# Gathered rows split one group later, sums over d apart, loads reordered at the start, dense layers begun in chunk 14

## Chip, cores and metric

One NeuronCore of a Trainium2 chip runs the whole program. The metric is the device time of one execution in microseconds (us), the median over the timed runs. TensorE (PE) does the matmuls, VectorE (DVE), ScalarE (ACT) and GpSimd (POOL) the rest; SyncE (SP) issues DMAs.

## What is computed

For 512 batch rows, 39 embedding tables give one row of 16 numbers each. A two-layer cross network (CIN) works on every batch row and every one of the 16 columns d, and its results are summed over d:

```python
e = stack([tbl_f[ids[:, f]] for f in range(39)])            # 512 x 39 x 16
z0 = einsum('bid,bjd->bdij', e, e)                           # 39*39 pairs
cur0 = relu(einsum('bdk,kl->bld', z0.reshape(...), W0))      # 128 outputs
next_h, direct0 = split(cur0, 2)                             # 64 and 64
z1 = einsum('bid,bjd->bdij', e, next_h)                      # 39*64 pairs
cur1 = relu(einsum('bdk,kl->bld', z1.reshape(...), W1))      # 128 outputs
z = sum(concat([direct0, cur1]), over d)                     # 192 features
h = relu(concat([z, dense_ctx]) @ W_top1 + b_top1)           # 208 -> 512
h = relu(h @ W_top2 + b_top2)                                # 512 -> 256
y = h @ W_top3                                               # 256 -> 1
```

## The kernel before

Everything is written by hand: each engine has its own stream of instructions, and semaphores order them. The batch is cut into 16 chunks of 32 rows; a chunk has 32 x 16 = 512 columns, and all matmuls have these as their moving dimension.

**Fetching a chunk.** GpSimd issues ten indirect DMAs per chunk (line 277; called gathers below) into `found[:, b, 2]`, one of three buffers. ACT makes a rounded copy (line 287) and VectorE the remainder (line 393); the two together are called the split of the chunk. SP then writes both and the plain values to a scratch tensor in DRAM (`lay_out`, line 198), reads them back with fields on partitions (`place`, `x_parts`, two DMAs, line 207), and spreads single rows over many partitions (`widen`, `x_wide`, line 217, 13 DMAs per chunk for groups 1 to 4). Each `widen` waits until the product that last read its buffer is done. The split of chunk c + 2 stands in group 0 of chunk c, on ACT and on VectorE.

**First layer of a chunk.** PE adds pairs of fields (`add_up`, line 482), ACT squares the sums (line 296), PE contracts the squares (`contract0`, line 499), in four pieces. ACT evicts the result (`evict0`, lines 303 to 307) into `h` (two copies) and `direct`; VectorE sums `direct` over d (`reduce0`, line 423).

**Second layer of a chunk**, in five groups g = 0 to 4, n = 5c + g counting them over all chunks. VectorE multiplies `h` with the chunk's fields (`multiply`, line 410): group 0 reads them from PSUM, where PE spread them (`spread_out`, line 512), groups 1 to 4 from `x_wide`. For all groups but 2, ACT rounds the product (`high_part`, line 320), VectorE subtracts to get the remainder (`low_part`, line 418), and PE does three passes: `contract1_hi` with two weights (lines 523, 524) and `contract1_lo` (line 531). Group 2 goes in full precision (`contract1_whole`, lines 538 and 542). `z`, `z_hi` and `z_lo` have three buffers. ACT evicts the sum (`evict1`, line 313) and VectorE sums it over d (`reduce1`, line 429). In group n VectorE does `multiply(n + 1)`, then `low_part(n)`; in group 4 both sums over d stand between them. Pieces of the first layer of the next chunks stand between the groups on PE.

**Dense layers.** Three matmul layers on the batch as columns: "early" the first 480, "late" the last 32. The early `hid1_of` (lines 560, 562) stand in groups 2 to 4 of the last chunk and wait for 15 sums over d, the early `hid2_of` (line 571) around the last `contract1_lo`, `y_of` (line 578) behind; then the late columns.

**Start.** ACT's queue issues four weight loads at once, SP's the ids, `w1` and the dense weights. PE fills the time until the first `x_parts` with 30 matmuls that nobody reads (`keep_busy`, line 489).

```python
            for c in range(1, CHUNKS - 1):
                if c + 2 < CHUNKS:
                    bring(c + 2)
                for i in range(len(WIDE)):
                    widen(c + 1, i)
```

## Time and profile before

| | |
|---|---|
| median of 3 timed runs | 441.9 us (439.06 to 444.56) |
| the profiled execution, timed | 437.52 us |
| its span in the profile | 435.7 us |
| granted TensorE clock, mean | 0.978 of full |
| PE busy | 400.6 us (92%) |
| DVE busy | 345.7 us (79%) |
| ACT busy | 226.0 us (52%) |
| POOL busy | 294.6 us (68%) |
| DMA, mean over the span | 185 GB/s |

A timeline row gives the start and the duration in us, the engine, the kernel's line, the operation, output and input, and in brackets how long the engine had been idle before it and what released it. "x4" means that four like instructions are merged. The profiled execution's 437.52 us are its 435.7 us of span and 1.8 us around it.

### The profile page before, as it was taken

What the parts mean: (1) busy time and instruction counts of PE and PEld (TensorE: products, weight loads), DVE (VectorE), ACT (ScalarE), POOL (GpSimd) and SP (SyncE); (2) the same over time, 40 slices, a digit from 0 to 9 for tenths busy, and PEclk for the clock granted to TensorE, in tenths of its full rate; (3) what the DMA queues carried; (4) which work ended last, traced back from release to release, by engine and by line L of the source; (5) the groups of instructions that cost most, each with busy time, mean ns of one, the idle gap of its engine ahead of it and who ended that gap; (6) DMA issues with size and microseconds to landing.
All of it is one profiled execution on the core that took longest, in us unless ns stands there. A gap on an engine that the chain in (4) does not pass through costs nothing.

```text
span 435.7 us, 4074 instructions
## 1 busy us (share of the span) xinstructions
PE 400.6 (92%) x1426; PEld 249.0 (57%) x1426; DVE 345.7 (79%) x196; ACT 226.0 (52%) x224; POOL 294.6 (68%) x164
## 2 busy tenths in 40 slices
PE   0868977999999899999999799999999999997897
PEld 0734634666666546666656356565656565664464
DVE  0305748799999798999998788999999989999800
ACT  3025544474738356564746273847475656553422
POOL 3778889888888888888888888898989800000000
PEclk9989998999999989999999799999999999999999
DMA  8384956496969497878879493959886888992000
GB/s 309 81 218 128 260 135 176 123 247 187 242 165 265 120 262 178 232 199 216 210 214 222 138 281 78 290 137 233 195 253 187 219 218 226 261 253 56 2 0 0
DMA packets 27862, 80.80 MB, mean 185 GB/s; under 512 B 7265, under 2 KB 16225, under 8 KB 20034
## 3 DMA queue, kind: packets, MB, share of 16 engines
q1 hardware_dynamic: 22146, 77.64, 65.9%
q0 software_dynamic: 5120, 1.32, 3.3%
q10 hardware_dynamic: 576, 1.58, 1.1%
q8 instruction: 11, 0.18, 0.2%
q14 instruction: 9, 0.07, 0.1%
HBM read 76.58 MB, written 3.93 MB: 185 GB/s over the span
## 4 chain that ended last, share of the span: by engine, by line
POOL 44%; PE 39%; issue 9%; DMA 3%; DVE 3%; ACT 0%; DVEq 0%
POOL found L277 44%; PE acc L499 7%; PE acc L531 6%; PE acc L524 5%; PE acc L523 5%; PE acc L542 5%; PE sums L482 3%; DMA found<-in_table_dram,rows_sb 2%; PE acc L538 2%; DVE z_lo L418 2%; PE spread L571 2%; DMA ids_sb<-in_ids_dram 1%; PE spread L512 1%; DVE z L410 1%; PE sums L560 1%
## 5 line engine op out<-in xcount | busy, mean ns | idle before, releaser
L277 POOL DMA_INDIRECT found<-in_table_dram,rows_sb x160 | 294.4, 1840 | 53.6 <-issue 48.5
L320 ACT ACTIVATE z_hi<-z 128x2048 fp32r<-128x2048 f32 x64 | 122.4, 1912 | 95.5 <-DVE z L410 95.5
L418 DVE TENSOR_TENSOR z_lo<-z,z_hi 128x2048 fp32r<-128x2048 f32 x64 | 145.8, 2279 | 0.0
L410 DVE TENSOR_TENSOR z<-x_wide,h 128x2048 f32<-128x2048 f32 x64 | 144.8, 2281 | 0.0
L499 PE MATMUL acc<-squares,w 128*128 128x512 f32 (+1 forms) x224 | 110.8, 612 | 0.0
L523 PE MATMUL acc<-z_hi,w_hi 128*128 128x512 f32 x256 | 107.3, 419 | 0.7 <-ACT cur L313 0.7
L524 PE MATMUL acc<-z_hi,w_lo 128*128 128x512 f32 x256 | 101.0, 394 | 0.0
L531 PE MATMUL acc<-z_lo,w_hi 128*128 128x512 f32 x256 | 84.3, 452 | 10.7 <-DVE z_lo L418 10.7
L296 ACT ACTIVATE squares<-sums 128x1024 f32<-128x1024 f32 x64 | 58.4, 913 | 35.5 <-PE sums L482 35.5
L531 PEld LDWEIGHTS acc<-z_lo,w_hi 128*128 128x128 f32 x256 | 47.9, 190 | 36.4 <-issue 15.2
L499 PEld LDWEIGHTS acc<-squares,w 128*128 128x128 f32 (+1 forms) x224 | 41.8, 192 | 28.8 <-issue 24.6
L523 PEld LDWEIGHTS acc<-z_hi,w_hi 128*128 128x128 f32 x256 | 48.7, 190 | 15.6 <-issue 4.1
L524 PEld LDWEIGHTS acc<-z_hi,w_lo 128*128 128x128 f32 x256 | 48.6, 190 | 13.8 <-issue 3.6
L542 PE MATMUL acc<-z,w_sb 128*128 128x512 f32 x96 | 46.6, 622 | 0.0
L482 PE MATMUL sums<-x_parts,select_sb 128*128 128x512 f32 x112 | 39.8, 425 | 6.8 <-DMA x_parts<-x_rows 4.4
L393 DVE TENSOR_TENSOR found<-found 128x160 fp32r<-128x160 f32 x16 | 5.2, 326 | 48.0 <-ACT found L287 48.0
L410 DVE TENSOR_TENSOR z<-spread,h 128x2048 f32<-128x2048 f32 x16 | 36.5, 2284 | 5.5 <-ACT h L304 3.0
L542 PEld LDWEIGHTS acc<-z,w_sb 128*128 128x128 f32 x96 | 17.5, 196 | 29.5 <-issue 29.5
L482 PEld LDWEIGHTS sums<-x_parts,select_sb 128*128 128x128 f32 x112 | 19.9, 190 | 15.9 <-issue 7.1
L313 ACT ACTIVATE cur<-acc 128x512 f32<-128x512 f32 x16 | 9.6, 597 | 33.0 <-PE acc L531 33.0
L429 DVE TENSOR_REDUCE feat_a<-cur 128x32 f32<-128x512 f32 x16 | 10.7, 669 | 12.3 <-ACT cur L313 12.3
L538 PE MATMUL acc<-z,w_sb 64*128 64x512 f32 x32 | 19.9, 703 | 0.0
(44 smaller groups left out, 134.0 us busy)
## 6 DMA issues: line engine op xcount, KB each, us to landing
x_wide<-x_rows SPq DMA_DIRECT2D x64, 512.0 KB, 8.1
x_wide<-x_rows SPq DMA_DIRECT2D x112, 256.0 KB, 9.9
x_parts<-x_rows SPq DMA_DIRECT2D x32, 128.0 KB, 2.6
x_rows<-found SPq DMA_DIRECT2D x16, 240.0 KB, 2.2
x_wide<-x_rows SPq DMA_DIRECT2D x16, 192.0 KB, 7.2
found<-in_table_dram,rows_sb POOLq DMA_INDIRECT x160, 7.6
w_sb<-in_w_dram SPq DMA_DIRECT2D x1, 1280.0 KB, 8.1
x_wide<-x_rows SPq DMA_DIRECT2D x16, 64.0 KB, 6.7
```

The lines of the kernel that those rows point to most:

```text
L277: pool.indirect_dma_start(out=found[:, b, 2, s * D:s * D + D], out_offset=None, in_=table, in_offset=bass.IndirectOffsetOnAxis(ap=rows_sb[ ...
L296: nc.scalar.activation(squares[rows, q % RING0, 0:n, :], sums[rows, 0:n, :], ACT.Square).then_inc(squared, 1)
L320: nc.scalar.activation(z_hi[:, n % RING], z[:, n % RING], ACT.Copy).then_inc(hi_done, 1)
L410: nc.vector.tensor_tensor(z[:, n % RING], x, h[:, c % 2, :].unsqueeze(1).to_broadcast([P, QUADS, N]), ALU.mult).then_inc(multiplied, 1)
L418: nc.vector.tensor_tensor(z_lo[:, n % RING], z[:, n % RING], z_hi[:, n % RING], ALU.subtract).then_inc(lo_done, 1)
L482: last = nc.tensor.matmul(sums[:, a, :], select_sb[:, t, :], x_parts[:, c % BUFS, :], start=True, stop=True)
L499: last = nc.tensor.matmul(acc0[:, :], w0[rows, t, :], squares[rows, q % RING0, a, :], start=(t == 0), stop=(t == T0 - 1))
L523: nc.tensor.matmul(acc1[:, :], w1_hi[:, t, :], z_hi[:, r, a, :], start=(t == 0), stop=False)
L524: last = nc.tensor.matmul(acc1[:, :], w1_lo[:, t, :], z_hi[:, r, a, :], start=False, stop=False)
L531: last = nc.tensor.matmul(acc1[:, :], w1_hi[:, slot1(g) + a, :], z_lo[:, r, a, :], start=False, stop=(g == G - 1 and a == QUADS - 1))
L538: nc.tensor.matmul(acc1[:, :], w1_sb[0:HALF, VT, :], z[0:HALF, r, 0, :], start=False, stop=False)
L542: last = nc.tensor.matmul(acc1[:, :], w1_sb[:, VT + a, :], z[:, r, a, :], start=False, stop=False)
```

## The change

1. **Ids first.** ACT waits for the ids before it issues its four weight loads. The row numbers of chunk 0 are computed by an instruction of their own, and GpSimd starts when that is done.
2. **Parts by two queues.** For chunk 0 the second half of `place` is issued by ACT instead of SP.
3. **First group in halves.** `multiply(0)` and `high_part(0)` are two instructions of 1024 columns each instead of one of 2048, and PE may start on the first half. `keep_busy` runs 36 matmuls instead of 30.
4. **Sums over d apart, splits in group 1.** `reduce0(c + 1)` stays in group 4 but goes behind the low part, `reduce1` goes to group 1, and the split of chunk c + 2 moves from group 0 to group 1 on ACT and VectorE. In chunks 0 and 1 ACT squares before it evicts, and `evict0(1)` comes a group earlier.
5. **Dense layers.** Early is now 448 columns (14 chunks), late 64. `hid1` has a buffer of its own. The early `hid1_of` start in the last group of chunk 14, one per group, then both `hid2_of`; `y_of(early)` comes right after the last `contract1_lo`.

```diff
-        early, late = slice(0, B - CB), slice(B - CB, B)
+        early, late = slice(0, B - 2 * CB), slice(B - 2 * CB, B)
...
-                place(c)
+                place(sp, c, 0)
+
+                if c:
+                    place(sp, c, 1)
...
+            act.wait_ge(ids_in, 16)
             act.dma_start(select_in, select).then_inc(select_in_done, 16)
...
             split(0)
+            place(act, 0, 1)
...
-            high_part(0)
+            act.wait_ge(half_multiplied, 1)
+            nc.scalar.activation(z_hi[:, 0, 0:2], z[:, 0, 0:2], ACT.Copy).then_inc(half_hi_done, 1)
+            act.wait_ge(multiplied, 1)
+            nc.scalar.activation(z_hi[:, 0, 2:], z[:, 0, 2:], ACT.Copy).then_inc(hi_done, 1)
             for c in range(CHUNKS):
                 for g in range(G):
                     n = G * c + g
+                    if g == 0 and c < 2:
+                        square(ND * (c + 1))
                     if g == 0 and c:
                         evict1(c - 1)
-                    if g == 0 and c < 2:
-                        square(ND * (c + 1))
...
-                    if g == (2 if c else 3) and c + 1 < CHUNKS:
+                    if g == 2 and c + 1 < CHUNKS:
                         evict0(c + 1)
-                    if n == 2:
-                        split(2)
-                    if g == 0 and 0 < c < CHUNKS - 2:
+                    if g == 1 and c + 2 < CHUNKS:
                         split(c + 2)
...
-                    if n == 3:
-                        split(2)
                     if n + 1 < G * CHUNKS:
                         multiply(n + 1)
-                    if g == G - 1 and c + 1 < CHUNKS:
-
-                        reduce0(c + 1)
-                        if c:
-                            reduce1(c - 1)
+                    if n == 2:
+                        split(2)
                     if is_v(n):
                         low_part(n)
                     if n == 0:
                         reduce0(0)
-                    if g == 0 and 0 < c < CHUNKS - 2:
+                    if g == 1 and 0 < c < CHUNKS - 2:
                         split(c + 2)
-                    if n == G * (CHUNKS - 1) + 1:
-                        reduce1(CHUNKS - 2)
+                    if g == 1 and c:
+                        reduce1(c - 1)
+                    if g == G - 1 and c + 1 < CHUNKS:
+                        reduce0(c + 1)
...
-                    if c == CHUNKS - 1 and g >= 2:
-                        for m in [[0], [1], [2, 3]][g - 2]:
+                    if n >= G * (CHUNKS - 1) - 1:
+                        m = n - G * (CHUNKS - 1) + 1
+                        if m < M1 // P:
                             hid1_of(m, early)
+                        else:
+                            hid2_of(m - M1 // P, early)
```

The order on VectorE in a chunk of the steady part. Before, from the two sums over d to the next product with `spread` (`found` is the split, `z_lo` a low part, `z` a product):

```order
L423 TENSOR_REDUCE feat_b<-direct 64x32
L429 TENSOR_REDUCE feat_a<-cur 128x32
L418 TENSOR_TENSOR z_lo<-z,z_hi 128x2048
L410 TENSOR_TENSOR z<-x_wide,h 128x2048
L418 TENSOR_TENSOR z_lo<-z,z_hi 128x2048
L393 TENSOR_TENSOR found<-found 128x160
L410 TENSOR_TENSOR z<-x_wide,h 128x2048
L418 TENSOR_TENSOR z_lo<-z,z_hi 128x2048
L410 TENSOR_TENSOR z<-x_wide,h 128x2048 x2
L418 TENSOR_TENSOR z_lo<-z,z_hi 128x2048
L410 TENSOR_TENSOR z<-spread,h 128x2048
```

The change:

```order
L420 TENSOR_TENSOR z<-spread,h 128x2048
L428 TENSOR_TENSOR z_lo<-z,z_hi 128x2048
L433 TENSOR_REDUCE feat_b<-direct 64x32
L420 TENSOR_TENSOR z<-x_wide,h 128x2048
L428 TENSOR_TENSOR z_lo<-z,z_hi 128x2048
L420 TENSOR_TENSOR z<-x_wide,h 128x2048
L428 TENSOR_TENSOR z_lo<-z,z_hi 128x2048
L403 TENSOR_TENSOR found<-found 128x160
L439 TENSOR_REDUCE feat_a<-cur 128x32
L420 TENSOR_TENSOR z<-x_wide,h 128x2048 x2
L428 TENSOR_TENSOR z_lo<-z,z_hi 128x2048
L420 TENSOR_TENSOR z<-spread,h 128x2048
```

The split (`found`) stood behind one product and two low parts after the sums; now it has one more product and one more low part ahead of it. The two sums over d no longer touch: one stands behind the low part of group 4, the other behind the split.

The order on ACT around the split of chunk 2 (`found`), from the last square of chunk 1 (`squares`, 64 rows) to the first work of chunk 1's groups. Before:

```order
L296 ACTIVATE squares<-sums 64x512
L320 ACTIVATE z_hi<-z 128x2048
L287 ACTIVATE found<-found 128x160
L320 ACTIVATE z_hi<-z 128x2048
L303 ACTIVATE h<-acc 64x512
L304 ACTIVATE h<-acc 64x512
L307 ACTIVATE direct<-acc 64x512
L320 ACTIVATE z_hi<-z 128x2048
L313 ACTIVATE cur<-acc 128x512
L296 ACTIVATE squares<-sums 128x1024 x3
```

The change:

```order
L302 ACTIVATE squares<-sums 64x512
L293 ACTIVATE found<-found 128x160
L326 ACTIVATE z_hi<-z 128x2048
L309 ACTIVATE h<-acc 64x512
L310 ACTIVATE h<-acc 64x512
L313 ACTIVATE direct<-acc 64x512
L326 ACTIVATE z_hi<-z 128x2048 x2
L302 ACTIVATE squares<-sums 128x1024
L319 ACTIVATE cur<-acc 128x512
```

The split of chunk 2 moved ahead of the rounding (`z_hi`) of group 3, the eviction of `h` ahead of the rounding of group 4, and a square ahead of the eviction of `cur`.

The end on PE, around and behind the last low pass (`acc1<-z_lo`). Matmuls that read `feat_b` and `feat_a` are `hid1_of`, those with `wt2_sb` `hid2_of`, those with `wt3_sb` `y_of`. Before:

```order
L571 MATMUL spread<-z,wt2_sb 128x480 x4
L531 MATMUL acc1<-z_lo,w1_hi 128x512 x4
L571 MATMUL spread<-z,wt2_sb 128x480 x4
L560 MATMUL sums<-feat_b,wt1b_sb 128x32
L562 MATMUL sums<-feat_a,wt1a_sb 128x32
L560 MATMUL sums<-feat_b,wt1b_sb 128x32
L562 MATMUL sums<-feat_a,wt1a_sb 128x32
L560 MATMUL acc0<-feat_b,wt1b_sb 128x32
L562 MATMUL acc0<-feat_a,wt1a_sb 128x32
L560 MATMUL spread<-feat_b,wt1b_sb 128x32
L562 MATMUL spread<-feat_a,wt1a_sb 128x32
L578 MATMUL spread<-z,wt3_sb 1x480 x2
```

The change, from its last low pass:

```order
L548 MATMUL acc1<-z_lo,w1_hi 128x512 x4
L595 MATMUL spread<-z,wt3_sb 1x448 x2
L577 MATMUL sums<-feat_b,wt1b_sb 128x64
L579 MATMUL sums<-feat_a,wt1a_sb 128x64
L577 MATMUL sums<-feat_b,wt1b_sb 128x64
L579 MATMUL sums<-feat_a,wt1a_sb 128x64
L577 MATMUL acc0<-feat_b,wt1b_sb 128x64
L579 MATMUL acc0<-feat_a,wt1a_sb 128x64
L577 MATMUL spread<-feat_b,wt1b_sb 128x64
L579 MATMUL spread<-feat_a,wt1a_sb 128x64
L588 MATMUL spread<-hid1_sb,wt2_sb 128x64 x8
L595 MATMUL spread<-z,wt3_sb 1x64 x2
```

Before, both early `hid2_of` (`wt2_sb`, 480 columns) stood around the last low pass; now neither is behind it, the late columns are 64 wide, and the early `y` (`wt3_sb`) has moved ahead of the late `hid1_of`.

## Rows read from the trace of the kernel before

**Rows 1.** Four stretches of the kernel: busy us (instructions) by engine, PEclk, DMA share, GB/s.

```profile
core 0: us, PE busy (x) PEld busy (x) DVE busy (x) ACT busy (x) POOL busy (x), PEclk, DMA share, GB/s
100.00:122.00 22.00, 22.00 (x83) 13.92 (x81) 21.00 (x13) 13.13 (x14) 19.26 (x10) 1.00 0.85 216
151.00:173.00 22.00, 20.15 (x68) 11.86 (x68) 19.70 (x12) 13.09 (x13) 18.34 (x13) 0.92 0.83 207
240.00:262.00 22.00, 18.84 (x60) 10.76 (x59) 18.12 (x11) 10.16 (x10) 18.26 (x12) 0.84 0.76 213
389.00:404.00 15.00, 10.88 (x44) 7.67 (x43) 15.00 (x10) 5.22 (x4) 0.00 (x0) 1.00 0.37 94
```

**Rows 2.** Timeline of chunk 8: start us, us, engine, line, operation [idle before].

```profile
231.43 7.19 POOL L277 DMA_INDIRECT found<-in_table_dram,rows_sb  x1 [0.30 <-issue]
241.85 0.34 ACT L287 ACTIVATE found<-found 128x160 fp32r<-128x160 f32 x1 [3.37 <-DMA found<-in_table_dram,rows_sb]
247.01 2.08 PE L531 MATMUL acc<-z_lo,w_hi 128*128 128x512 f32 x4 [3.16 <-DVE z_lo L418]
```

**Rows 3.** Timeline of GpSimd and VectorE, chunks 9 and 10.

```profile
270.73 1.90 POOL L277 DMA_INDIRECT found<-in_table_dram,rows_sb  x1 [0.30 <-issue]
280.78 0.94 POOL L277 DMA_INDIRECT found<-in_table_dram,rows_sb  x1 [0.30 <-issue]
281.13 0.67 DVE L429 TENSOR_REDUCE feat_a<-cur 128x32 f32<-128x512 f32 x1
281.72 2.27 DVE L418 TENSOR_TENSOR z_lo<-z,z_hi 128x2048 fp32r<-128x2048 f32 x1
282.03 7.19 POOL L277 DMA_INDIRECT found<-in_table_dram,rows_sb  x1 [0.30 <-issue]
```

**Rows 4.** Timeline of VectorE and GpSimd, chunk 0 and chunk 4.

```profile
44.85 0.67 DVE L423 TENSOR_REDUCE feat_b<-direct 64x32 f32<-64x512 f32 x1
45.45 2.27 DVE L410 TENSOR_TENSOR z<-x_wide,h 128x2048 f32<-128x2048 f32 x1
46.05 6.90 POOL L277 DMA_INDIRECT found<-in_table_dram,rows_sb  x1 [0.30 <-issue]
148.73 2.80 POOL L277 DMA_INDIRECT found<-in_table_dram,rows_sb  x1 [0.30 <-issue]
```

**Rows 5.** Timeline of the start.

```profile
4.97 0.32 DVE L434 TENSOR_TENSOR rows_sb<-ids_sb 128x160 uint32<-128x160 int32 x1 [4.97 <-DMA ids_sb<-in_ids_dram]
15.51 7.88 PE L489 MATMUL acc<-select_sb 128*128 128x512 f32 x30
26.07 0.73 PE L482 MATMUL sums<-x_parts,select_sb 128*128 128x512 f32 x2 [2.69 <-DMA x_parts<-x_rows]
```

**Rows 6.** Timeline of chunks 0 and 1.

```profile
59.07 0.34 ACT L287 ACTIVATE found<-found 128x160 fp32r<-128x160 f32 x1 [3.54 <-DMA found<-in_table_dram,rows_sb]
65.17 2.29 DVE L410 TENSOR_TENSOR z<-spread,h 128x2048 f32<-128x2048 f32 x1 [1.00 <-ACT h L304]
73.10 0.73 PE L482 MATMUL sums<-x_parts,select_sb 128*128 128x512 f32 x2 [1.60 <-ACT squares L296]
```

**Rows 7.** Timeline of the way from a split to its users, chunk 9.

```profile
267.08 0.32 DVE L393 TENSOR_TENSOR found<-found 128x160 fp32r<-128x160 f32 x1 [1.71 <-ACT found L287]
269.79 1.19 SPq L207 DMA_DIRECT2D x_parts<-x_rows  x2
277.30 0.74 PE L482 MATMUL sums<-x_parts,select_sb 128*128 128x512 f32 x2
```

**Rows 8.** The page's part 6: issues by form, times, KB each, us to landing.

```profile
x_parts<-x_rows SPq DMA_DIRECT2D x32, 128.0 KB, 2.6
```

**Rows 9.** Timeline of the end.

```profile
388.90 2.29 DVE L410 TENSOR_TENSOR z<-spread,h 128x2048 f32<-128x2048 f32 x1 [0.30 <-PE spread L512]
424.24 3.38 PE L571 MATMUL spread<-z,wt_sb 128*128 128x480 f32 x8
433.57 0.59 ACT L386 ACTIVATE y_sb<-spread 1x512 f32<-1x512 f32 x1 [0.31 <-PE spread L578]
```

More of the change, by code:

```diff
@@ L187, in uses, with place @@
             return c // BUFS + 1
+        def place(queue, c, half):
+            b = c % BUFS
+            queue.wait_ge(rows_out[b], 16 * uses(c))
+            start = x_rows[b, half, 0, 0:1]
+            queue.dma_start(x_parts[half:P:2, b, :].bitcast(F32),
+                            bass.AP(start.tensor, start.offset, [[N, 2 * STEP], [STEP * N, QUADS], [1, N]])
+                            ).then_inc(placed[b], 16)
         block = ctx.enter_context(nc.Block())
@@ L331, in hid2_act @@
             def hid2_act(m, batch):
+                if m == 0 and batch == early:
+                    act.wait_ge(contracted1, G * CHUNKS - 2)
                 act.wait_ge(hid2_done, m + 1 + (M2 // P if batch == late else 0))
@@ L650, in _ @@
                 hid1_of(m, late)
-            y_of(early)
             for m in range(M2 // P):
```

57 lines of the change are left out of this document (30 added, 27 removed).

## Prediction

> **What bounds the kernel now.** I read the chain of waits in order of time first. It runs through GpSimd's gathers in the first half of the span and through PE in the second, so neither alone is the bound. I then cut the span into stretches of a chunk's length. In an undisturbed one PE is busy for all 22.00 us of 22, VectorE for 21.00 and GpSimd for 19.26 [rows 1]. All three are nearly full, and PE sets the pace. In two other stretches PE is idle for 22 − 20.15 = 1.85 and 22 − 18.84 = 3.16 us, and its mean granted clock is 0.92 and 0.84, that is, for part of them it ran at 1.2 instead of 2.4 GHz. At half clock for 16% and 32% of 22 us it loses another 1.8 and 3.5 us against full speed. Together the two stretches lose 10.3 us [rows 1].
>
> What happened in the second of them the timeline says. A gather, the last of its chunk, took 7.19 us from 231.43. The split of the chunk waited for it on ACT until 241.85, with 3.37 us idle. VectorE could not go past its half of the split, so the low part behind it was late, and PE stood 3.16 us at its low pass [rows 2]. The steady part is thus bound by PE, and now and then by GpSimd.
>
> Why GpSimd is late is the next thing to see. In the regular case a gather takes 1.90 us: it starts inside a VectorE instruction with two inputs in SBUF and ends 0.9 us after the next boundary between two of them. But the gather from 282.03, which begins 0.31 us into a low part that follows the two sums over d, takes 7.19 us, and passes only when VectorE is through with three such instructions [rows 3]. I shall call that a lock-out. The same was seen in chunk 0, where one sum stood ahead of a product: 6.90 us for a gather that began 0.60 us into the product. A gather that began shortly into a product behind a split was let through at the next boundary (2.80 us) [rows 4]. One lock-out costs GpSimd about 7.2 + 0.3 − 2 x 2.2 = 3 us against regular passage.
>
> The Trainium skill (SBUF — State Buffer, "Who interferes with whom") says that a VectorE instruction with two SBUF inputs contends with a GpSimd instruction that reads SBUF, and that the second blocks until the first finishes. The row agrees with the contention and not with its length: 7.19 us are three instructions, not one. By the rule alone no gather would be late in either kernel, and the whole 10.3 us would have had another cause.
>
> **The change, part by part.** The sum is made against the profiled execution's 437.5 us. The timed runs lie at 439.06 to 444.56, median 441.9, so up to 4.4 us above it.
>
> *Start: −2.2.* The ids land and the row numbers start at 4.97 us [rows 5], with four loads of ACT's queue beside them. Alone a transfer of 128 x 170 numbers, 85 KB, should need no more than `x_parts` did, 2.6 us for 128 KB [rows 8]; issued at 0.7 it lands at 3.3 or before, so 1.7 us are won, and the small row-number instruction gives back most of 0.32 us [rows 5]. Two queues save half of the 1.19 us that SP needs to issue the two parts [rows 7], 0.6. GpSimd and the first parts so come about 2 and 2.6 us earlier. But PE is then in its filler: 30 matmuls take 7.88 us from 15.51, so 36 take 9.5 and end at 25.0 or later, since ACT's loads, on which they wait, are issued 2 us later [rows 5]. PE begins the sums at 25 to 27 instead of 26.07. It gains there only the clock: it had been idle for 2.69 us [rows 5] and ran the first squares' matmuls slower. That is worth 1 to 2 us. The halves let ACT and PE begin about 1.1 us earlier (half a product of 2.29), while VectorE, which has its next product anyway, gains nothing. What carries the term to the end is the gather of chunk 2, which is awaited until 59.07 [rows 6]; it moves by the 2 us that GpSimd starts earlier. Bounds: 0 (the loads keep the ids as late as before) and −5 (its lock-out [rows 4] is also missed).
>
> *Chunks 0 and 1: −3.3.* From the split of chunk 2 on: `h` of chunk 1 is evicted before the rounding of group 4, so the product with `spread` loses its 1.00 us of waiting; the sum over d now stands behind the low part, another 0.6; together the low part is 1.6 us earlier. PE then stood 1.60 us for a square that ACT could not do because an eviction stood ahead of it [rows 6]; they change places. Against it, the rounding of group 3 is now behind the split: it used to be done early and now comes 0.34 + 1.9 us after 59.07. That takes PE's wait to an earlier place and does not lengthen it, for the low pass behind it waits for VectorE anyway. Bounds +1 and −5.
>
> *Steady part: −8.* A late gather now hits later. Before, the split had one product and one low part behind it that PE needed; now these stand ahead, which is 2 x 2.2 = 4.4 us of room. The next limit is `x_parts`: split at 267.08, parts issued from 269.79 to 270.98, landed 2.6 us after the second issue at about 273.0, used at 277.30 [rows 7, 8]. So the split may be up to 4.3 us later in PE's time before PE waits. On the other side PE is earlier against GpSimd by the 3.3 us just won, which leaves some 1 us; so the term rests on GpSimd's speed. Beside the sums over d and the product from PSUM a gather takes 0.94 us, and with the 0.30 between two it is one each 1.25 [rows 2, 3]. If no lock-out comes, a chunk has nine or ten passages in 22 us and PE is never stopped: −10.3. If one comes in each chunk, its 3 us are more than the 1 us that VectorE has free (22.00 − 21.00 [rows 1]), GpSimd falls behind by 1 to 2 us a chunk as it did, and perhaps 5 of the 10 us stay. I take −8 as nearer to the first: what stood ahead of the lock-outs, two sums back to back, is gone. `x_wide` is issued up to 4.4 us later too; no row of the waits shows VectorE waiting for it, so I count nothing, with +1 per chunk, +13, as the far end.
>
> *End: −4.* In the last chunk PE is busy only 10.88 of 15 us [rows 1], as the first layer's pieces have run out. From 388.90 to 424.24, where the last low pass ends, are 35.3 us, 4.1 of them idle. Now the early dense layers stand there whole: the second early `hid2_of` (3.38 us for eight records [rows 9]) is added, the narrower early columns (448 of 480) take off a fifteenth of 6.8 + 3.4 + 3.4 (sixteen records for `hid1_of`, at the same 0.42), that is 0.9, and about 1.6 of idle stay, for two evictions. That is 31.2 + 3.4 − 0.9 + 1.6 = 35.3, so the last low pass ends where it did. Behind it were 433.57 − 424.24 = 9.3 us to the last copy [rows 9]. Of these 3.4 go (the `hid2_of`), and the early `y`, four records or 1.7 us, now covers the eviction and the sum over d, some 1.3 us that the `hid2_of` covered before: it gives back nothing, and at best 1 us more is won. About −4 in all. Bounds −1.5 and −6.
>
> Sum: 437.5 − 2.2 − 3.3 − 8 − 4 = 420.0. For the timed runs I add 1, not 4.4, because part of their spread should be the stalls that go: **421 us**.
>
> The Trainium skill (DMA: Bandwidth & Descriptors, "Issuing engines are not separate DMA queues") says that DMAs from several engines share the same DMA engines and interleave, and that a second issuer only saves issue time. No row shows two issuers for parts. By it the second queue is worth the 0.6 us of issue and nothing of the transfer; I have counted just that.
>
> **Rivals.**
>
> *A. Gathers stay behind as before* (424 to 433). The lock-outs come once a chunk at the new place, behind the lone sum of group 1. Half of the 10.3 us stay and sometimes more: 421 + 5 = 426 to 430. For it: the start 0.35 us into the product is about where the locked ones were (0.31 to 0.60). Against it: a split ran just before, as in the case that passed.
>
> *B. No change within 2%* (434 to 450). Same place, but the lock-out is longer by an instruction (two products and a low part stand there) and takes two passages of ten. GpSimd then lacks 2 x 1.25 us of VectorE's idle time a chunk, of which 1.0 is there: 1.5 x 12 = 18 us, and a half clock now and then: 421 + 18 = 439.
>
> *C. Slower: two lock-outs a chunk.* Both lone sums are followed by instructions with two SBUF inputs, and the one case of before with a lone sum locked out [rows 4]. By the same arithmetic (a gather passes at the sum's start, takes 0.9, the next begins 0.3 later, 0.60 into the product) it would recur every chunk. Then only about five gathers pass while VectorE is busy, the other five need 1.25 us of idle each: 6.3 − 1.0 = 5.3 us a chunk, over 12 chunks 63: 484 us; if half the chunks do so, 452. It decides from about 2.5 us a chunk. Against it: idle time of VectorE ahead of the product, 1 us in PE's rhythm, takes the gather out of the bad phase.
>
> *D. The change of order does not do what it says:* the split is released not by its place but by the gather, and everything else is hidden. Then start and end alone remain: 437.5 − 6 = 431; I count it with A.
>
> **Chances.** Forecast (412 to 424) 0.40, A with D 0.23, B 0.20, C 0.17. The measurement tells about 2% from no change, that is 433.1 and 450.7. Faster by over 2%: 0.40 + 0.23 = 0.63, less 0.01 for D's edge: 0.62. Within: 0.21. Slower: 0.17. The range 412 to 446 leaves out C and a little at the low end. The likeliest case's own range is 412 to 424.
>
> **What would show it.** First row numbers at about 3.4 us. The filler's end after 25 us and full clock behind it. Granted clock 1.00 and PE busy for the whole of every 22 us stretch between 80 and 360, with the gathers' mean near 1.6 us and no 7 us gather right behind a sum over d. The splits' waits for gathers gone, the last product with `spread` at about 370 us, and 6 instead of 9.3 us from the last low pass to the last copy. The forecast is wrong if a 7 us gather stands in each chunk (A, B), if there are two or one of 10 us (C), or if VectorE begins to wait for `x_wide` or PE for `x_parts`.

## The result, and the profile after

The changed kernel takes 453.4 us (median of 4 runs, 451.9 to 458.5), the kernel before in the same comparison 442.0 (439.1 to 444.6). The ratio is 1.028 with a 95% interval of 1.020 to 1.037: slower, by 11.4 us; whether by more than 2% the interval just leaves open. Its profiled execution was timed at 458.5 us, with a span of 456.7; the difference to before's span of 435.7 is 21.0 us.

The page of the changed kernel, parts 1, 2, 4 and 5 (busy us and share of the span; the granted clock in tenths; the chain; then line, engine, operation, busy and mean ns, idle time before):

```profile
PE 403.5 (88%) x1432; PEld 256.0 (56%) x1432; DVE 347.2 (76%) x198; ACT 227.1 (50%) x225; POOL 330.2 (72%) x164
...
PEclk9999999899998999899999879999997999899999
...
POOL 70%; PE 14%; issue 11%; DMA 3%; POOLq 2%; ACT 0%; DVE 0%; SPq 0%
...
L283 POOL DMA_INDIRECT found<-in_table_dram,rows_sb x160 | 330.0, 2062 | 51.3 <-issue 48.5
```

The chain that ended last now runs through GpSimd for 70% of the span. The same 160 gathers take 330.0 us in place of the 294.4 of before, 2062 ns each in place of 1840.

Its waits, largest first (engine, line and tile, what it waited for: us in total, times, longest):

```profile
ACT found L293 <- DMA found<-in_table_dram,rows_sb: 64.1, 14, 9.2
...
PE sums L497 <- DMA x_parts<-x_rows: 34.7, 12, 6.9
...
DVE z_lo L428 <- ACT z_hi L326: 8.6, 14, 1.2
```

ACT waits for the rows of 14 splits, and PE then stands at the first `add_up` that needs them, 34.7 us in all. Before, PE stood 10.7 us for low parts and 4.4 us for `x_parts`. So the wait has a new place, and is more than twice as long. Two stretches of the changed kernel (columns as in [rows 1]):

```profile
151.00:173.00 22.00, 22.00 (x82) 13.91 (x81) 20.06 (x13) 13.25 (x13) 20.17 (x7) 1.00 0.79 216
...
327.00:349.00 22.00, 17.64 (x54) 10.56 (x53) 16.27 (x11) 9.30 (x10) 18.80 (x11) 0.84 0.62 164
```

In the first, as good as before's best, PE is busy throughout, but GpSimd passes only 7 gathers where [rows 1] has 10. In the second the debt is paid: PE stands for 22 − 17.64 = 4.4 us and runs at a mean clock of 0.84.

How it comes about, GpSimd and VectorE at the end of chunk 6 of the changed kernel:

```profile
217.19 1.89 POOL L283 DMA_INDIRECT found<-in_table_dram,rows_sb  x1 [0.30 <-issue]
218.19 0.67 DVE L433 TENSOR_REDUCE feat_b<-direct 64x32 f32<-64x512 f32 x1
218.78 2.27 DVE L420 TENSOR_TENSOR z<-x_wide,h 128x2048 f32<-128x2048 f32 x1
219.39 9.10 POOL L283 DMA_INDIRECT found<-in_table_dram,rows_sb  x1 [0.30 <-issue]
```

A gather that waits for the end of the low part passes when the sum of `direct` starts and is done 0.90 us later. The next begins 0.30 us after that, which is always 0.60 to 0.61 us into the product behind the sum, and here it is locked out: it takes 9.10 us. Of the 16 gathers over 4 us of this trace (before: 11), 14 began just there; they took 4.7 to 9.3 us, that is, they passed at the second, third or fourth boundary between two VectorE instructions.

Where the 21.0 us lie is read from the starts of the products with `spread`: that of chunk 2 at 85.79 (before 90.38), that of chunk 15 at 416.01 (before 388.90). Up to the first: −4.6. Between the two: 330.2 for 298.5, +31.7. From the second to the end of the span: 40.7 for 46.8, −6.1. The start and the end did what they were to do, and the steady part lost 32 us.

### The profile page after: what moved, and what is told of

Same layout as the page of the kernel before. It is cut to its first block, busy times and chain, and to the rows that moved or that the text cites. A ratio compares the mean times of both kernels' runs of the same rounds, so it can differ in the third digit from the quotient of the medians.

```text
span 456.7 us, 4090 instructions
## 1 busy us (share of the span) xinstructions
PE 403.5 (88%) x1432; PEld 256.0 (56%) x1432; DVE 347.2 (76%) x198; ACT 227.1 (50%) x225; POOL 330.2 (72%) x164
## 4 chain that ended last, share of the span: by engine, by line
POOL 70%; PE 14%; issue 11%; DMA 3%; POOLq 2%; ACT 0%; DVE 0%; SPq 0%
POOL found L283 70%; PE acc L540 2%; PE acc L541 2%; PE acc L548 2%; PE spread L588 2%; POOLq L85 2%; DMA found<-in_table_dram,rows_sb 1%; PE acc L559 1%; PE acc L514 1%; DMA x_parts<-x_rows 1%; PE sums L497 1%; DMA x_rows<-found 0%; PE sums L577 0%; PE acc L555 0%; DMA ids_sb<-in_ids_dram 0%
## 5 line engine op out<-in xcount | busy, mean ns | idle before, releaser
L283 POOL DMA_INDIRECT found<-in_table_dram,rows_sb x160 | 330.0, 2062 | 51.3 <-issue 48.5
L540 PE MATMUL acc<-z_hi,w_hi 128*128 128x512 f32 x256 | 111.6, 436 | 0.0
L514 PE MATMUL acc<-squares,w 128*128 128x512 f32 (+1 forms) x224 | 108.3, 601 | 0.0
L541 PE MATMUL acc<-z_hi,w_lo 128*128 128x512 f32 x256 | 105.0, 410 | 0.0
L548 PE MATMUL acc<-z_lo,w_hi 128*128 128x512 f32 x256 | 82.1, 442 | 0.0
L497 PE MATMUL sums<-x_parts,select_sb 128*128 128x512 f32 x112 | 42.5, 452 | 35.6 <-DMA x_parts<-x_rows 34.7
L540 PEld LDWEIGHTS acc<-z_hi,w_hi 128*128 128x128 f32 x256 | 51.3, 201 | 15.4 <-issue 4.2
L541 PEld LDWEIGHTS acc<-z_hi,w_lo 128*128 128x128 f32 x256 | 51.0, 199 | 14.9 <-issue 3.7
L293 ACT ACTIVATE found<-found 128x160 fp32r<-128x160 f32 x16 | 5.4, 337 | 64.1 <-DMA found<-in_table_dram,rows_sb 64.1
L420 DVE TENSOR_TENSOR z<-spread,h 128x2048 f32<-128x2048 f32 x15 | 34.3, 2284 | 1.4 <-PE spread L527 1.4
L319 ACT ACTIVATE cur<-acc 128x512 f32<-128x512 f32 x16 | 9.6, 598 | 36.5 <-PE acc L548 36.5
```

The lines of the kernel that those rows point to most:

```text
L283: pool.indirect_dma_start(out=found[:, b, 2, s * D:s * D + D], out_offset=None, in_=table, in_offset=bass.IndirectOffsetOnAxis(ap=rows_sb[ ...
L420: nc.vector.tensor_tensor(z[:, n % RING], x, h[:, c % 2, :].unsqueeze(1).to_broadcast([P, QUADS, N]), ALU.mult).then_inc(multiplied, 1)
L497: last = nc.tensor.matmul(sums[:, a, :], select_sb[:, t, :], x_parts[:, c % BUFS, :], start=True, stop=True)
L514: last = nc.tensor.matmul(acc0[:, :], w0[rows, t, :], squares[rows, q % RING0, a, :], start=(t == 0), stop=(t == T0 - 1))
L540: nc.tensor.matmul(acc1[:, :], w1_hi[:, t, :], z_hi[:, r, a, :], start=(t == 0), stop=False)
L541: last = nc.tensor.matmul(acc1[:, :], w1_lo[:, t, :], z_hi[:, r, a, :], start=False, stop=False)
```

## Experiments

**Which part loses the time?** Three versions of the changed kernel, each with part of edit 4 undone. The first puts both sums together ahead of the low part and the splits into group 0:

```diff
+                    if g == G - 1 and c + 1 < CHUNKS:
+                        reduce0(c + 1)
+                        if 0 < c < CHUNKS - 2:
+                            reduce1(c - 1)
                     if is_v(n):
                         low_part(n)
...
-                    if g == 1 and 0 < c < CHUNKS - 2:
+                    if g == 0 and 0 < c < CHUNKS - 2:
                         split(c + 2)
```

> The changed kernel with part 4 undone in the steady part: both sums over d stand together ahead of the low part again, and the splits in group 0; all other parts stay. Theory 1 (each lone sum ahead of a product gives GpSimd a lock-out): one 7.2 us gather a chunk at most, as before the change, and 428 to 435 us, faster than the kernel before by start and end. Theory 2 (the loss comes from the start, the halves, or the dense layers begun early): it stays near 450. Theory 3 (the late split starves PE of x_parts by itself): 428 to 435 as well.

The second keeps the sums apart and puts the splits back into group 0; the third, run a second time, keeps the splits in group 1 and puts the sums together:

> Only the splits go back to group 0; the sums over d stay apart. Theory 1: lock-outs of 6.9 us and more behind the sum of group 4 stay in nearly every chunk, and the late gathers hit 4 us earlier, so at least as slow as the changed kernel: 450 to 462 us. Theory 3 (the late split is the cause): 430 to 440.

> Only the sums over d go back together ahead of the low part; the splits stay in group 1. Theory 1: the number of lock-outs falls back to one a chunk of 7.2 us, mean of a gather near 1.85 us, and 420 to 430 us. Theory 3: PE still waits some 30 us in all for x_parts, 445 to 455.

> The kernel with sums together and splits in group 1 once more, since its times lay apart on the chip before (424 and 445 to 453). Theory 1: 420 to 430 us wherever ACT and VectorE are not stopped in the first 80 us; one long gather a chunk or fewer.

The first took 446.4 us (432.6 to 448.8), the second 457.5 (ratio to before 1.026, 1.018 to 1.034), the third 446.0 (424.1 to 452.6) and 439.5 (424.8 to 445.7); the kernel before took 447.7 beside the first three and 442.2 beside the last. In the profiles of the first three ACT and VectorE stood still between 39 and 84 us for up to 18 us with nothing that the profile shows them to wait for, so their medians say little. The fastest runs of the first and third, 432.6, 424.1 and 424.8, lie where theory 1 had them. Their gathers say more: 12 long ones of 4.7 us behind the lone sum in the second, 12 of 7.0 to 7.2 in the first, and only 3 and 4 in the two profiles of the third, though up to 18.4 us long. That speaks against the sums apart and not against the late splits; the times alone don't prove it.

**What the kernel needs when GpSimd stops nobody.** Both kernels with 5 gathers of 10 per chunk; the other rows are zeros, so half of the fetched fields are left out:

```diff
-                for s in range(SLOTS):
+                for s in range(SLOTS // 2):
```

> The changed kernel with 5 of the 10 gathers of each chunk; the other rows are left as zeros. Nothing else changes. Theory 1: GpSimd is never late, PE sets the pace: 410 to 420 us, and no wait for x_parts. Theory 3: the wait of PE for x_parts stays at half or more of its 34.7 us, 435 or more.

> The kernel before with 5 of its 10 gathers per chunk (the other rows stay zero, so five fields in ten of each row are not fetched). GpSimd then stops nobody, and what is left is what the other engines need. The changed kernel with the same cut took 413.6. Theory (start, chunks 0 and 1 and end were about rightly priced, and the loss lies in the gathers alone): 413.6 plus 2.2 for the start, 1 to 3 for chunks 0 and 1, 4 for the end = 421 to 423. Rival (those parts brought nothing either): 412 to 416. The gather whose lock-out closes chunk 0 goes in both.

Measured: 413.6 for the changed kernel and 426.3 for the kernel before, one run each. With half of the gathers the change is worth 12.7 us; 7 to 9 were expected. The gathers are not free here: the changed kernel still has 16 long ones among its 80. But GpSimd now has room for them, and PE waits only 2.1 us for `x_parts`. So a lock-out costs time where GpSimd is nearly full, and next to nothing here.

**Both sums ahead of the product with `spread`.** This product reads PSUM and has one input in SBUF only:

```diff
-                    if g == 1 and c:
-                        reduce1(c - 1)
-                    if g == G - 1 and c + 1 < CHUNKS:
-                        reduce0(c + 1)
+                    if g == G - 2:
+                        if c + 1 < CHUNKS:
+                            reduce0(c + 1)
+                        if c:
+                            reduce1(c - 1)
```

> The changed kernel with both sums over d moved ahead of the product with spread, at the end of group 3; splits stay in group 1. Behind the sums then stands a product that reads PSUM, not one with two SBUF inputs. Theory 1 (a lock-out needs a sum directly ahead of an instruction with two SBUF inputs): hardly any gather over 4 us, mean about 1.6 us, no wait of PE for x_parts, 412 to 424 us. Theory 2 (gathers are slow because VectorE is denser, wherever the sums stand): mean over 1.85 us and over 435 us.

> The same with the splits in group 0. Theory 1: the place of the split matters only when gathers are late, so the same as with splits in group 1 within 4 us. If late splits by themselves cost something, this is faster by 5 us or more.

> The version with both sums ahead of the product with `spread` (425.3) and with 26 instead of 36 filler matmuls at the start. 10 of them at 0.256 us are 2.6 us. Theory (the filler held PE up past the landing of the parts and PE sets the pace from there on): adding begins at about 25 instead of 27.4 us, and the time falls by 1.5 to 2.5 us, to 423 to 424. Rival 1 (the gathers of chunk 2 set the start, whatever PE does): within 0.5 us of 425.3. Rival 2 (PE is then idle before the parts land and drops to half clock): 427 or more, and a granted clock below 1 between 25 and 35 us.

With the splits in group 1 it took 425.3 us (ratio 0.952, 0.945 to 0.959), with only 2 long gathers: 1 us above the expected range, and faster than both kernels. With the splits back in group 0: 433.1, and 12 lock-outs of 6.6 to 7.2 us, most of them in the low part behind that product. With 26 filler matmuls: 439.4 (427.5 to 447.3), and 10 long gathers of up to 11.6 us in the profile. The last two missed what was expected. PE did begin at 24.79 instead of 26.68 us, but then it stood 3.66 us at the parts of chunk 1, so the start gained nothing. So a product that reads PSUM does not protect what stands behind it. It may be that in such an order PE's lead over GpSimd decides whether a gather is caught; two runs below bear on that.

**The sum of group 4 done twice.** A dummy `tensor_reduce` of `direct` into a tile that nobody reads stands ahead of the real one, which shifts the phase of the next gather by 0.6 us:

> The changed kernel with the sum of group 4 done twice, once more into a tensor that nobody reads: 0.6 us more work on VectorE a chunk. Theory 1 with the phase (a gather locks out if it begins about 0.3 to 0.6 us into the instruction behind a sum): the gather that began 0.61 us into the product now begins at its start and passes at the next boundary, so fewer gathers over 4 us, and 425 to 440 us, faster than the changed kernel although it does more. Theory without phase (any lone sum ahead of a product): 453 or more, with as many long gathers.

Measured 466.8 us (ratio 1.058, 1.050 to 1.066), with 14 long gathers, nine of them of 9.7 us and one of 17.1, that start 0.01 to 0.02 us into the product. That a lock-out needs 0.3 to 0.6 us into the instruction has fallen.

**One instruction moved.** The sum of `direct` of the changed kernel ahead of the product with `spread`, nothing else:

```diff
+                    if g == G - 1 and c + 1 < CHUNKS:
+                        reduce0(c + 1)
                     if n + 1 < G * CHUNKS:
                         multiply(n + 1)
...
-                    if g == G - 1 and c + 1 < CHUNKS:
-                        reduce0(c + 1)
```

> The changed kernel with one instruction moved: the sum over d of group 4 (reduce0) stands ahead of the product with `spread`, which has only one input in SBUF, instead of behind the low part and ahead of the product with `x_wide`, which has two. Everything else stays. Theory (a gather that starts shortly behind a lone sum is locked out if the instruction behind the sum has two inputs in SBUF): the lock-outs behind reduce0 go, those few behind the other sum stay, at most 5 gathers over 4 us instead of 16, mean gather 1.70 to 1.80 instead of 2.06, time 423 to 432. Rival (what costs is that the sums are apart at all, or that they fall into group 1 and group 4): still a long gather in most chunks, 445 to 458.

Four runs: 421.7, 423.1, 442.3 and 459.5 us. The profiled one is the fastest, with 2 long gathers and a mean of 1698 ns. The theory holds for two runs and not for the others. Whether a lead or a lag of GpSimd decides between them, the next two were to tell: the changed kernel with 5 gathers each in chunks 3 to 5 (half of their rows are stale), and the version just above with 10 more gathers, into a spare tile, ahead of chunk 5's:

```diff
-                for s in range(SLOTS):
+                for s in range(SLOTS // 2 if 3 <= c < 6 else SLOTS):
```

> The changed kernel, but chunks 3, 4 and 5 are fetched with 5 gathers each instead of 10 (the other rows keep what their buffers held), which puts GpSimd some 30 us ahead of PE. Theory 1 (the order alone makes the lock-outs): they are there from chunk 6 on as in the changed kernel, at 0.6 us into the product behind the sum of group 4, the lead is used up within about 15/2 chunks or so (some 3 us of lag a chunk), and the time is 455 less part of 30, at 425 to 445. Theory 2 (two modes: once PE leads, VectorE has idle time and the phase is never met): hardly a gather over 4 us behind chunk 6, and 415 to 422.

> The version with the sum of `direct` ahead of the product with `spread` (its profiled run 421.7), with 10 more gathers ahead of chunk 5's, into a buffer that nobody reads: GpSimd falls some 20 us behind once. Theory 1 (no lock-outs in this order, wherever GpSimd stands): a gather needs about 1.7 us, 17 us a chunk against 22, so the lag is made up within four chunks and the time is 421.7 plus what PE waits once, 10 to 20: 430 to 442. Theory 2 (a kernel that has once fallen behind stays there): long gathers from chunk 5 to the end, 450 or more, as in the single run of 459.5.

The changed kernel with its lead took 445.8 us, 8 less than without it, though 15 gathers are left out: it has 18 long gathers, ten of them later than 160 us, up to 9.3 us each. In this order the lead doesn't keep them away, and theory 2 falls; the time lies 1 us above theory 1's. The good order with the lag took 451.6, with seven long gathers. The first three, at 47.00, 62.84 and 89.69 us, came before the extra gathers, which begin at 101.61; so the lag can't be all of it. The last three stand at 175.74, 226.34 and 277.51. One of them:

```profile
223.88 0.67 DVE L441 TENSOR_REDUCE feat_b<-direct 64x32 f32<-64x512 f32 x1
224.48 2.27 DVE L428 TENSOR_TENSOR z<-spread,h 128x2048 f32<-128x2048 f32 x1
225.09 0.94 POOL L291 DMA_INDIRECT found<-in_table_dram,rows_sb  x1 [0.30 <-issue]
226.34 12.24 POOL L291 DMA_INDIRECT found<-in_table_dram,rows_sb  x1 [0.32 <-issue]
226.68 2.27 DVE L436 TENSOR_TENSOR z_lo<-z,z_hi 128x2048 fp32r<-128x2048 f32 x1
```

The sum of `direct`, the product with `spread` and the low part follow each other with no pause on VectorE, and the gather that begins 0.34 us before the low part takes 12.24 us, six boundaries. In the profiled run of the same order without the lag, VectorE stands 0.94 us for ACT ahead of that low part in seven chunks, and the gathers there pass in 2.0 us. From 283 us on PE was again busy for 22.00 us of 22 and no gather was long, so neither theory was right, and what starts and ends such a spell stays open. Both are single runs.

**The place or the sum?** I counted in all profiles up to here, but for these last two, how gathers fared that began within an instruction with two SBUF inputs:

```
instruction, and what stood ahead of it       locked out of all that began in it
product with x_wide behind sum of direct      56 of 59
product with x_wide behind sum of cur          2 of 47
product with x_wide behind a low part          0 of 140
product with x_wide behind a split             0 of 97
product with x_wide behind another one         7 of 144
low part behind product with x_wide            0 of 320
low part behind both sums, direct ahead       25 of 46
```

The two behind the sum of `cur` began right behind another long gather, and so did four of the seven; all seven are in the version with half of the gathers. The expectation below has 3 of 48, which the traces don't bear out. Low parts were locked out where the sum of `direct` stood one to three instructions ahead, as in [rows 3], but not always.

Both sums are `tensor_reduce` of 512 columns and take 0.67 us. One works on 64 partitions, the other on 128. So the two were exchanged in the changed kernel:

```diff
-                        reduce1(c - 1)
-                    if g == G - 1 and c + 1 < CHUNKS:
-                        reduce0(c + 1)
+                        reduce0(c)
+                    if g == G - 1 and 0 < c < CHUNKS - 2:
+                        reduce1(c - 1)
```

> The changed kernel with its two sums over d exchanged: in group 4, behind the low part, the sum of `cur` (128 partitions) stands alone, in group 1, behind the split, the sum of `direct` (64 partitions). In all traces so far 56 of 59 gathers that began in a product with `x_wide` behind the sum of `direct` were locked out, and 3 of 48 behind the sum of `cur`; but the first always stood behind a low part and the second behind a split. Theory P (the place: what stands ahead of the sum decides): the lock-outs stay in group 4, now behind the sum of `cur`, one in most chunks, time 445 to 458. Theory W (the sum itself, 64 partitions, decides): none behind the sum of `cur`, one in most chunks in group 1 behind the sum of `direct`; time again 440 to 458, but at the other place. Theory S (both are needed, the sum of `direct` and no split ahead): hardly any, 423 to 432.

It took 446.7 us in ten runs (ratio 1.010, 1.005 to 1.014). None of its long gathers began behind the sum of `cur` in group 4; 12 of 13 began during the sum of `direct` in group 1 or up to 0.62 us into the product behind it, with the split ahead of the sum; the other is chunk 0's, behind the same sum. One chunk of it, each sum with the gather behind it:

```profile
314.43 0.68 DVE L439 TENSOR_REDUCE feat_a<-cur 128x32 f32<-128x512 f32 x1
315.63 2.49 POOL L283 DMA_INDIRECT found<-in_table_dram,rows_sb  x1 [0.31 <-issue]
...
326.42 0.67 DVE L433 TENSOR_REDUCE feat_b<-direct 64x32 f32<-64x512 f32 x1
327.64 6.88 POOL L283 DMA_INDIRECT found<-in_table_dram,rows_sb  x1 [0.30 <-issue]
```

Twelve gathers began 0.60 to 0.61 us into the product behind the sum of `cur` in group 4, where the changed kernel has its lock-outs; all took 2.5 us. Theory P fell, theory W stood: it is the sum, not its place.

**The sum over 128 partitions.** In both kernels, and in the version with one instruction moved:

```diff
-        direct = sb("direct", [HALF, N])
+        direct = sb("direct", [P, N])
+        feat_w = sb("feat_w", [P, B])
...
-                nc.vector.tensor_reduce(feat_b[0:HALF, c * CB:c * CB + CB],
+                nc.vector.tensor_reduce(feat_w[:, c * CB:c * CB + CB],
...
+            for batch, count in ((early, CHUNKS - 2), (late, CHUNKS)):
+                pool.wait_ge(reduced0, count)
+                nc.gpsimd.tensor_copy(feat_b[0:HALF, batch], feat_w[0:HALF, batch]).then_inc(copied, 1)
```

> The changed kernel with the sum of `direct` over 128 partitions instead of 64 (the upper 64 hold zeros; GpSimd copies the lower half of the sums for the dense layers when its gathers are done). The order of all instructions stays, and so does the time of the sum (0.67 us for 64 and for 128 partitions in the traces). Theory W (the lock-outs need the sum over 64 partitions: 137 of the 151 long gathers of all profiles stand within three VectorE instructions behind it, and most others right behind another long one): no gather over 4 us, except what stands behind other causes, mean 1.6 to 1.75, time 418 to 428. Rival (it is the data or the wait of that sum, or chance of the phase, and not its partitions): 445 to 458 with a long gather at 0.6 us into the product of most chunks, as in the changed kernel.

> The kernel before with the same edit. Theory W: its ten lock-outs of 7.2 us go too; it keeps its longer start and end (with half of the gathers it took 426.3, the changed kernel 413.6): 427 to 433. Rival: 438 to 446 with 9 to 11 long gathers.

> The changed kernel with the sum of `direct` over 128 partitions and ahead of the product with `spread`. Theory W: no lock-outs and no second mode: all runs between 416 and 426. Rival (the slow runs of that order, 442 and 459, come from somewhere else): one run in two again above 435.

| | median, us | range | ratio to before | gathers over 4 us | mean gather, ns |
|---|---|---|---|---|---|
| changed kernel, wide sum | 416.9 | 415.2 to 419.8 | 0.942 (0.933 to 0.952) | 0 | 1761 |
| kernel before, wide sum | 429.2 | 425.0 to 430.0, and one of 1400.9 | 0.970 (0.959 to 0.980) | 0 | 1580 |
| moved by one, wide sum | 416.6 | 415.3 to 420.8 | 0.944 (0.934 to 0.953) | 0 | 1669 |

Every lock-out is gone in all three. The first is 1 us below its expected range, the second within it (what it lost are the 11 long gathers of before, nine of them of 7.2 us), and the four runs of the third lie within 5.5 us of each other, where those with the narrow sum lay 38 apart. The run of 1400.9, and one of 577.9 of the kernel before beside it, have no profile and stay unexplained. The changed kernel with the wide sum, end of chunk 7, to be read against the rows of the changed kernel above:

```profile
224.15 0.68 DVE L438 TENSOR_REDUCE feat_w<-direct 128x32 f32<-128x512 f32 x1
224.74 2.28 DVE L425 TENSOR_TENSOR z<-x_wide,h 128x2048 f32<-128x2048 f32 x1
225.35 2.50 POOL L285 DMA_INDIRECT found<-in_table_dram,rows_sb  x1 [0.30 <-issue]
226.94 2.28 DVE L433 TENSOR_TENSOR z_lo<-z,z_hi 128x2048 fp32r<-128x2048 f32 x1
```

The gather begins at the same 0.61 us into the same product, and passes at the next boundary: 2.50 in place of 9.10 us. All 13 gathers of this trace that began there took 2.48 to 2.50. Its page and one stretch:

```profile
PE 392.3 (95%) x1432; PEld 248.3 (60%) x1432; DVE 346.5 (84%) x199; ACT 226.6 (55%) x225; POOL 286.7 (69%) x166
...
PE 83%; POOL 5%; DMA 5%; issue 3%; DVE 2%; ACT 1%; SPq 0%; DVEq 0%; ACTq 0%
...
L285 POOL DMA_INDIRECT found<-in_table_dram,rows_sb x160 | 281.7, 1761 | 51.3 <-issue 48.5
```

```profile
216.00:238.00 22.00, 22.00 (x82) 14.00 (x81) 21.07 (x13) 13.22 (x14) 18.95 (x11) 1.00 0.84 213
```

The chain is PE's for 83%, and a stretch has 11 gathers at full clock. The last run takes back the width alone and keeps the tiles and the copies:

```diff
-                nc.vector.tensor_reduce(feat_w[:, c * CB:c * CB + CB],
-                                        direct[:, :].rearrange("p (b d) -> p b d", d=D), AX.X,
+                nc.vector.tensor_reduce(feat_w[0:HALF, c * CB:c * CB + CB],
+                                        direct[0:HALF, :].rearrange("p (b d) -> p b d", d=D), AX.X,
```

> The version with the wide sum, with that one instruction put back to 64 partitions; the new tile for its result, the larger `direct`, the cleared half and GpSimd's two copies stay. Theory W (the number of partitions alone): the lock-outs are back, 14 to 18 gathers over 4 us, most of them 0.6 us into the product behind that sum, mean about 2.0 to 2.1, time 448 to 458. Rival (it was the other place of the tiles in SBUF, or the copies): hardly a long gather and 415 to 420, as with the wide sum.

```profile
190.46 0.67 DVE L438 TENSOR_REDUCE feat_w<-direct 64x32 f32<-64x512 f32 x1
191.06 2.27 DVE L425 TENSOR_TENSOR z<-x_wide,h 128x2048 f32<-128x2048 f32 x1
191.67 9.09 POOL L285 DMA_INDIRECT found<-in_table_dram,rows_sb  x1 [0.30 <-issue]
...
L285 POOL DMA_INDIRECT found<-in_table_dram,rows_sb x160 | 332.6, 2079 | 51.2 <-issue 48.4
```

459.1 us in two runs (ratio 1.044, 1.037 to 1.052), 1 us above the expected range, with 16 long gathers, 14 of them behind that sum. The partition count of one instruction makes 42 us, a ratio to the kernel before of 1.044 in place of 0.942.

## Why the prediction was wrong

The forecast was 421 us, with a range of 412 to 446; the measurement was 453.4.

**The result is nearest to rival C, which I gave 0.17.** Its arithmetic was right to a hundredth: a gather passes at the sum's start, takes 0.9, the next begins 0.30 later, 0.60 into the product. It recurred behind 14 of the 16 sums of `direct`. Its price was too high and its count too: 5.3 us for each of 12 chunks with two lock-outs, 63 us, or 452 in all if half of the chunks did so. Only in two chunks did a second one follow, behind the other sum, and the steady part lost 31.7 + 8 = 39.7 us against my forecast, 3.3 a chunk. That the measured 453.4 lies next to the 452 is luck: the 452 has half of the chunks at 5.3 us, and the runs show nearly all of them at 3.3.

**The step that failed** is in the steady part: "I take −8 as nearer to the first: what stood ahead of the lock-outs, two sums back to back, is gone." The traces before held both cases: the seven-microsecond gather behind two sums [rows 3], and that of chunk 0 behind the sum of `direct` alone [rows 4]. And chunk 1 of before had a lone sum too, ahead of a low part, which I overlooked:

```profile
67.38 0.67 DVE L423 TENSOR_REDUCE feat_b<-direct 64x32 f32<-64x512 f32 x1
67.78 7.68 POOL L277 DMA_INDIRECT found<-in_table_dram,rows_sb  x1 [0.30 <-issue]
67.97 2.27 DVE L418 TENSOR_TENSOR z_lo<-z,z_hi 128x2048 fp32r<-128x2048 f32 x1
```

What all of them had in common was the sum over 64 partitions, not the pair. I weighed one row of the lone sum less than nine of the pair. The change left that sum and put it ahead of a product in every chunk, so the case of [rows 4] became the rule: 31.7 us more in the steady part where I had 8 less.

**The argument against C failed too.** I held that idle time of VectorE takes the gather out of the bad phase. It can't: a gather that is waiting passes at a boundary, and the boundary is the start of the sum itself. The phase is set anew each time, which is why the 14 lie at 0.60 to 0.61 us into their products. The run in which GpSimd was given a lead agrees: the lock-outs came nevertheless.

**The steady term has the right size without lock-outs, but not by what I changed.** From the product of chunk 2 to that of chunk 15 the changed kernel with the wide sum takes 374.30 − 83.52 = 290.8 us. Against before's 298.5 this is −7.7; I had −8, and −10.3 for a PE that is never stopped. The kernel before with the wide sum takes 376.31 − 87.74 = 288.6, which is −9.9. So the new order brings nothing in the steady part once the gathers are free, and is even 2.2 us longer there in these two profiles: the whole gain is that of the lock-outs. That my −8 and the −7.7 agree is therefore partly luck. `x_wide`, far end +13, made VectorE wait 0.5 us in all.

**Start and chunks 0 and 1: −5.5 forecast, −4.6 measured** at the product of chunk 2, made up otherwise than I said. The row numbers came at 2.82 (I said about 3.4), the gathers 2.3 us earlier (I said 2). But the mix of the weights began at 15.19 instead of 12.40, since the loads behind the ids landed later, and then:

```profile
18.33 9.21 PE L504 MATMUL acc<-select_sb 128*128 128x512 f32 x36
27.38 0.61 PE L497 MATMUL sums<-x_parts,select_sb 128*128 128x512 f32 x2
...
53.61 0.34 ACT L293 ACTIVATE found<-found 128x160 fp32r<-128x160 f32 x1 [0.33 <-DMA found<-in_table_dram,rows_sb]
```

The filler ended the wait for the parts at 27.38, later than the 25 to 27 that I gave and than before's 26.07; at full clock (1.00 granted up to 38 us, 0.86 before) PE then caught up, and the first product of chunk 0 came at 38.08 for 38.24. So "1 to 2 us" of the clock held, and PE's start gained nothing beyond it. What the start did win is my far end: GpSimd's 2.3 us put one more gather ahead of the lock-out of chunk 0, and the split of chunk 2 came at 53.61 for 59.07 [rows 6], 5.5 us earlier. Of the three waits of [rows 6] ACT's is down to 0.33 us, VectorE's is gone, and PE stands 0.19 us for the square.

**End: −4 forecast, −6.1 to the end of the span.** In the changed kernel (PE and ACT; the stretch has the columns of [rows 1]):

```profile
448.54 0.60 ACT L319 ACTIVATE cur<-acc 128x512 f32<-128x512 f32 x1 [3.03 <-PE acc L548]
...
454.52 0.59 ACT L396 ACTIVATE y_sb<-spread 1x512 f32<-1x512 f32 x1 [0.36 <-PE spread L595]
```

```profile
416.00:448.00 32.00, 32.00 (x111) 20.61 (x112) 23.28 (x12) 11.76 (x12) 0.00 (x0) 1.00 0.31 72
```

From the last low pass to the last copy are 6.0 us, as forecast (9.3 before). The rest was mis-sized: I left 1.6 us of idle on PE for two evictions and took the stretch up to the last low pass as unchanged at 35.3. PE had no idle time there at all, and it took 32.5. That leaves 1.2 us less work than I had added up (31.2 + 3.4 − 0.9 = 33.7), for which I have no account.

**The other rivals.** A had the right count of one lock-out a chunk, but a price of half of 10.3 us. B had the longer lock-out and 18 us for 12 chunks; measured were 39.7. Both were low in price, and both had the lock-out behind the sum of group 1, where it came behind that of group 4. D, start and end alone, fell as a forecast of 431. But it describes what is left where nothing is locked out: the two profiles with the wide sum differ by 8.1 us, −4.2 up to the product of chunk 2, +2.2 between, −6.1 behind; the medians differ by 12.3 (429.2 − 416.9), and with half of the gathers it is 12.7. The Trainium skill's rule of contention (SBUF — State Buffer, "Who interferes with whom"), by which a blocked instruction waits for the other one to finish, would have had no late gather in either kernel. By the same section `tensor_reduce` never contends on trn2; the sum itself indeed lets a gather through, but by the last run's 459.1 against 416.9 us its number of partitions decides what happens in the instructions behind it.

## What to carry to other kernels

Before a change puts an instruction into a new neighbourhood in every iteration, look for the one place in the trace where that neighbourhood already exists, and price the change by it, even if it is a single row. Group the long instances of an operation by what ran ahead of them on the other engine, by exact tile and partition count; here that count pointed at a 64-partition reduce. If GpSimd issues indirect DMAs beside VectorE work with two SBUF inputs, try the short VectorE instructions on all 128 partitions. Here that was worth 36.5 us in the changed kernel and 13.3 in the one before.

## What the runs showed of the hardware

- Behind a `tensor_reduce` on 64 partitions (0.67 us) a gather that waits for VectorE instructions with two SBUF inputs mostly does not pass at the next boundary, but at the second to ninth: 4.7 to 18.4 us. It is not so each time: 3 of 59 passed in 2.5 us at the same 0.60 to 0.61 us into the product, and 21 of 46 in the low part behind both sums; what decides is open. On 128 partitions (0.68 us) it passes at the next (2.5 us from 0.61 us into the product); none of 480 gathers in the three kernels with the wide sum took over 4 us. Why is open. That any VectorE instruction on 64 partitions does it was not tried, nor other counts.
- A product with one input in PSUM lets a gather through (0.94 us) but does not end that state: the gather of 226.34 above was caught in the low part behind one. Of the 155 long gathers in the sixteen profiles taken before the wide sum was tried, 141 began in or within three VectorE instructions of the sum of `direct` (the expectation above has 137 of 151: it leaves one profile out), and 11 of the other 14 right behind another long one; 3, of 4.5 to 5.0 us in the version with half of the gathers, stay unexplained.
